# A gated feed-forward kernel with row-wise selection: the residual of blocks 0 to 2 added partly by accumulating transfers

## The reference

```
s_h = silu(xn @ Wg_a.T);  the 1376 entries of a row smallest in |s_h| are set to 0
s   = (s_h * (xn @ Wu_a.T)) @ Wd_a.T
g   = silu( (silu(xn @ Wg_b.T) * (xn @ Wu_b.T)) @ Wd_b.T )
out = x + s * g
```

## Time and profile before

| | us |
|---|---|
| median of 3 runs (lowest, highest) | 2768.76 (2768.42, 2770.05) |
| the profiled execution | 2768.99 |
| its span on the core | 2767.2 |

### The profile page before, as it was taken

How to read it: one execution, slowest core, us unless ns; L and a number is a source line. 1 busy time by engine, 2 the same in 40 slices (tenths; PEclk the granted TensorE clock), 3 DMA queues, 4 the chain that set the end, 5 groups by cost and what they waited for, 6 DMA issues and landing times.

```text
span 2767.2 us, 31398 instructions
## 1 busy us (share of the span) xinstructions
PE 2745.4 (99%) x12204; PEld 2275.1 (82%) x12204; DVE 2298.5 (83%) x3002; ACT 1350.6 (49%) x1386; POOL 408.4 (15%) x185
## 2 busy tenths in 40 slices
PE   9999999999999999999999999999999999999999
PEld 7878888878788888888878888888887888888887
DVE  6776989999976798998986688999898667999971
ACT  4235988332445477731145457771115546776110
POOL 5565443074400000000020000000011000000000
PEclk9999999999999999999999999999999999999999
DMA  6898888579766555556666655555666664555564
GB/s 234 313 337 286 294 288 278 211 265 362 256 195 192 179 192 197 192 190 223 245 205 191 193 179 197 189 191 197 243 220 205 193 196 180 188 193 198 191 232 169
DMA packets 135097, 614.28 MB, mean 222 GB/s; under 512 B 12752, under 2 KB 12752, under 8 KB 89168
## 3 DMA queue, kind: packets, MB, share of 16 engines
q1 hardware_dynamic: 134992, 612.94, 63.2%
HBM read 492.31 MB, written 120.59 MB: 221 GB/s over the span
## 4 chain that ended last, share of the span: by engine, by line
PE 88%; DVE 8%; DMA 2%; issue 1%; ACT 0%; POOL 0%; SPq 0%; DVEq 0%; POOLq 0%; ACTq 0%
PE ps L634 27%; PE ps L854 19%; PE ps L883 11%; PE ps L882 11%; PE ps L884 11%; PE ps L784 2%; PE ps L785 2%; PE ps L787 2%; DMA w_raw<-w_a 1%; DVE prods L1364 1%; DVE key_buf L1635 1%; DVE hid_ring L1407 1%; DVE xnT L1355 1%; DVE key_buf L1643 1%; DVE ranks L1605 1%
## 5 line engine op out<-in xcount | busy, mean ns | idle before, releaser
L634 PE MATMUL ps<-w_split,hid_ring 128*128 128x512 f32 x4096 | 933.7, 390 | 3.7 <-DVE hid_ring L1407 2.1
L634 PEld LDWEIGHTS ps<-w_split,hid_ring 128*128 128x128 f32 x4096 | 769.1, 188 | 167.2 <-issue 5.4
L1390 DVE TENSOR_SCALAR_CACHE_REDUCE ranks<-key_buf,cand 128x2752 int16<-128x2752 f32 x248 | 762.8, 3076 | 5.8
L968 ACT ACTIVATE signs_row<-key_buf,cand 128x2752 bf16<-128x2752 f32 x248 | 642.2, 2590 | 191.7 <-DVE cand L1399 182.2
L884 PE MATMUL ps<-xnT,w_split 128*128 128x512 f32 x1376 | 535.3, 389 | 0.0
L883 PE MATMUL ps<-xnT,w_split 128*128 128x512 f32 x1376 | 535.3, 389 | 0.0
L882 PE MATMUL ps<-xnT,w_split 128*128 128x512 f32 x1376 | 535.3, 389 | 0.0
L1216 POOL TENSOR_TENSOR w_split<-w_raw,w_split 128x1024 fp32r<-128x1024 f32 (+3 forms) x142 | 309.7, 2195 | 354.3 <-ACT w_split L935 134.6
L884 PEld LDWEIGHTS ps<-xnT,w_split 128*128 128x128 f32 x1376 | 258.3, 188 | 53.8
L882 PEld LDWEIGHTS ps<-xnT,w_split 128*128 128x128 f32 x1376 | 258.3, 188 | 53.7
L883 PEld LDWEIGHTS ps<-xnT,w_split 128*128 128x128 f32 x1376 | 258.3, 188 | 53.2
(11 more groups left out here) (146 smaller groups left out, 2884.6 us busy)
## 6 DMA issues: line engine op xcount, KB each, us to landing
w_split<-split SPq DMA_DIRECT2D x272, 1024.0 KB, 4.8
split<-w_split SPq DMA_DIRECT2D x72, 1024.0 KB, 6.7
w_raw<-w_a SPq DMA_DIRECT2D x97, 512.0 KB, 3.7
w_raw<-t_dram SPq DMA_DIRECT2D x81, 512.0 KB, 3.3
w_raw<-w_b SPq DMA_DIRECT2D x42, 512.0 KB, 4.8
t_dram<-t_buf SPq DMA_DIRECT2D x20, 1024.0 KB, 8.5
w_extra_raw<-t_dram SPq DMA_DIRECT2D x39, 512.0 KB, 3.3
w_extra_raw<-w_a SPq DMA_DIRECT2D x33, 512.0 KB, 3.6
```

Of the source, the lines that this page charges most:

```text
L634: ins = pe.matmul(ps[:, 2 * t + half, :], h, w[:, half * TB:(half + 1) * TB], start=(first and n == 0), stop=last and stop)
L968: act.activation(signs_row[:, :], keys[:, t, :], ACT.Sign, bias=cand_f[:, t:t + 1], scale=-1.0, accum_out=counts[:, t:t + 1]).then_inc(act ...
L1390: dve.tensor_scalar(ranks[:, :], keys[:, t, :], cand_f[:, t:t + 1], 0.0, ALU.is_lt, ALU.add, accum_out=counts[:, t:t + 1]).then_inc(sel_st ...
```

## The change

For blocks 0 to 2: x of row tiles 2 and 3 is no longer loaded into `x_res`, but copied by SP from `x` straight to its rows of `out` in DRAM. GpSimd makes the sums of row tiles 0 and 1 as before, and for row tiles 2 and 3 starts two transfers that add `silu_g` to what lies in `out` (`accum_op=ALU.add`, new semaphore `added`). DVE's `last_outputs` and SP's stores of row tiles 2 and 3 are gone. In block 3 nothing is computed in another way.

The homes of the token sums change: P6 goes to home 3 (now never written by x in these blocks), P5 to home 0, P7 to home 2, P3 to home 1. Their waits change with them: `s_hi(0)` waits for nothing of the block's end; `s_hi(1)` for GpSimd's two sums; `s_hi(2)` for the two stores; `s_hi(3)`, which stood with `s_hi(2)` at a = 5, stands at a = 7 and waits for both accumulating transfers.

```diff
+S_HOME = (3, 0, 2, 1)
...
-                    sp.dma_start(x_res[:, t, :], x_v[b][:, t, :]).then_inc(xres_landed[t], 16)
+                    dst = out_v[b][:, t, :] if b < NB - 1 and t >= STAGE else x_res[:, t, :]
+                    sp.dma_start(dst, x_v[b][:, t, :]).then_inc(xres_landed[t], 16)
...
                         if a == W_RING - 1:
                             store(b - 1, 0)
                             store(b - 1, 1)
-                        elif W_RING <= a < W_RING + 2:
-                            store(b - 1, a - W_RING + 2)
...
-                        return s_split[:, which, part, 2 * (1 - pair) + n, at_col:at_col + P]
+                        return s_split[:, S_HOME[which], part, 2 * (1 - pair) + n, at_col:at_col + P]
...
                             if a == 1:
-                                act.wait_ge(out_ready, (b - 1) * OUT_POOL + STAGE)
                                 s_hi(0)
                             elif a == 2:
-                                act.wait_ge(out_ready, (b - 1) * OUT_POOL + OUT_POOL)
-                                act.wait_ge(out_last, b)
+                                act.wait_ge(out_ready, b * STAGE)
                                 s_hi(1)
                             elif a == 5:
-                                act.wait_ge(stored, b * (16 * NT) + 16)
+                                act.wait_ge(stored, b * (16 * STAGE) + 16)
                                 s_hi(2)
+                            elif a == 7:
+                                act.wait_ge(added, b * (16 * (NT - STAGE)))
                                 s_hi(3)
...
-                for t in range(OUT_POOL if b < NB - 1 else OUT_POOL - 1):
+                for t in range(STAGE):
                     pool.wait_ge(xres_landed[t], b * 16 + 16)
                     pool.wait_ge(ad_free, b * NT + (NT + t + 1))
                     pool.tensor_tensor(x_res[:, t, :], x_res[:, t, :], silu_g[:, t, :], ALU.add).then_inc(out_ready, 1)
+                for t in range(STAGE, NT) if b < NB - 1 else ():
+                    pool.wait_ge(xres_landed[t], b * 16 + 16)
+                    pool.wait_ge(ad_free, b * NT + (NT + t + 1))
+                    pool.dma_start(out_v[b][:, t, :], silu_g[:, t, :], accum_op=ALU.add).then_inc(added, 16)
...
                     w_lows(b, 3, 4)
-                    last_outputs(b - 1, OUT_POOL)
```

More of the change, by code:

```diff
@@ L396, in build @@
         stored = sem("stored")
+        added = sem("added")
         sel_init = sem("sel_init")
@@ L557, in between @@
                     t = m - AD0 - 4 - NT
-                    sp.dma_start(x_res[:, t, :], x_v[b][:, t, :]).then_inc(xres_landed[t], 16)
+                    dst = out_v[b][:, t, :] if b < NB - 1 and t >= STAGE else x_res[:, t, :]
+                    sp.dma_start(dst, x_v[b][:, t, :]).then_inc(xres_landed[t], 16)
             def store(b, t):
[L561 to L564, removed]
+                sp.wait_ge(out_ready, b * STAGE + (t + 1))
                 sp.dma_start(out_v[b][:, t, :], x_res[:, t, :]).then_inc(stored, 16)
@@ L601, in _ @@
                 if t < OUT_POOL - 1:
-                    sp.wait_ge(out_ready, (NB - 1) * OUT_POOL + (t + 1))
+                    sp.wait_ge(out_ready, (NB - 1) * STAGE + (t + 1))
                 else:
-                    sp.wait_ge(out_last, (NB - 1) * (NT - OUT_POOL) + 1)
+                    sp.wait_ge(out_last, 1)
                 sp.dma_start(out_v[NB - 1][:, t, :], x_res[:, t, :]).then_inc(stored, 16)
@@ L607, in _ @@
                 cols = slice(half * TB, (half + 1) * TB)
-                sp.wait_ge(out_last, (NB - 1) * (NT - OUT_POOL) + (half + 2))
+                sp.wait_ge(out_last, half + 2)
                 sp.dma_start(out_v[NB - 1][:, NT - 1, cols], x_res[:, NT - 1, cols]).then_inc(stored, 16)
-            sp.wait_ge(stored, 16 * (NT * NB + 1) + 16)
+            sp.wait_ge(added, (NB - 1) * (16 * (NT - STAGE)))
+            sp.wait_ge(stored, 16 * ((NB - 1) * STAGE + NT + 1) + 16)
         @block.tensor
@@ L1032, in s_hi @@
                     act.wait_ge(s_raw, (b - 1) * 4 + 4)
-                    act.activation(s_split[:, which, 0, :, :].rearrange("p k n -> p (k n)"), prods[:, which, 0:H], ACT.Copy).then_inc(s_high, 1)
+                    act.activation(s_split[:, S_HOME[which], 0, :, :].rearrange("p k n -> p (k n)"), prods[:, which, 0:H], ACT.Copy).then_inc(s_high, 1)
                 if not first_block:
@@ L1071, in run @@
                         hi(b, m)
-                act.wait_ge(stored, b * (16 * NT) + 16)
+                act.wait_ge(stored, b * (16 * STAGE) + 16)
+                if not first_block:
+                    act.wait_ge(added, b * (16 * (NT - STAGE)))
                 def silu_b(c, rows=P, tiles=1):
@@ L1462, in s_lo @@
                     dve.wait_ge(s_high, (b - 1) * 4 + (which + 1))
-                    dve.tensor_tensor(s_split[:, which, 1, :, :].rearrange("p k n -> p (k n)"), prods[:, which, 0:H],
-                                      s_split[:, which, 0, :, :].rearrange("p k n -> p (k n)").bitcast(F32), ALU.subtract).then_inc(s_ready, 1)
+                    dve.tensor_tensor(s_split[:, S_HOME[which], 1, :, :].rearrange("p k n -> p (k n)"), prods[:, which, 0:H],
+                                      s_split[:, S_HOME[which], 0, :, :].rearrange("p k n -> p (k n)").bitcast(F32), ALU.subtract).then_inc(s_ready, 1)
                 def w_keys(s, tiles):
```

## The result

The changed kernel takes 2776.9 us, the median of 8 runs (2774.96 to 2778.66), against 2769.01 us (2768.24 to 2770.52) for the kernel before: 7.9 us slower, ratio 1.0024 with a 95% interval of 1.0015 to 1.0034. The forecast was 2764.0 us, with a range up to 2772.6 us: the measured time lies beyond it.

The account below looks back on a forecast made before the run. TensorE, busy 99% of the span, bounds the kernel; only its idle time at block starts, held by DVE's order, can be won. Gains of 1.88 + 1.44 + 1.44 = 4.8 us from 2768.76 give 2764.0 us, range 2762.5 to 2772.6.

Parts of the forecast that it names:

- the place of what could be won, and its size in blocks 2 and 3: At block starts, where TensorE idles: DVE's order makes P6 late; 1.44 us to win at each of blocks 2 and 3.
- the 4.8 forecast: Whole gain at the starts of blocks 1 to 3: 1.88 + 1.44 + 1.44 = 4.8 us.
- the 1.88 us of block 1: Start of block 1, from P1 on: P6 is 1.88 us late, all of it to be won.
- nothing waits for the accumulating transfers: Block starts: only `s_hi(3)` on ACT waits for the two adding transfers, which land in time; cost 0.
- 5.8 to 17 us was bounded, 19.6 allowed: Block 2 start: both adding transfers take 5.8 to 17 us; they must land within 19.6 us of GpSimd's second sum.
- Rival B: Before P2: adding transfers land too late, `s_hi(3)`, `s_lo(3)` and TensorE wait; slower, 2770 to 2795 us; chance 0.11.
- Rival A: Block starts: GpSimd's issue blocks DVE's subtractions as a sum does; 2766.4 us, or 2772.6 if both issues do; chance 0.18.
- the copies in DRAM cost nothing to be seen: Copying x to out instead of loading it to SBUF: taken as 0, with bounds of 0 to 3 us.
- "Their traffic ... Cost 0": Block 2 start: adding transfers read 1 MB more, but weight loads may take over three times as long; cost 0.
- The allowance: Block 2 start: weight tile 8, asked for at about 1415.8, has its raw data wanted at 1427.0.
- Rival C: Before P6: another late arrival, say slower weight loads from two extra reads, replaces DVE's chain; nothing won, 2768.8 us; chance 0.08.
- T1: Theory for the experiments: adding makes transfers dear in DMA engine time, delaying weight loads they meet; for e4, 2770 to 2775 us.

Follow-up runs that it names:

- e2: Changed kernel, but GpSimd starts no transfer for row tiles 2 and 3, only counts the semaphore up; 2766.84 us, ratio 0.9986 to the kernel before.
- e6: Kernel before, but DVE sums row tiles 2 and 3 behind weight tile 5's low part; later stores, new homes, no adding transfers; 2767.88 us, ratio 0.9989.
- e10: The kernel of e6 run again, unchanged, on another chip's comparison with the kernel before; 2766.76 us, ratio 0.9990.
- e7: The kernel before, run again unchanged for a second profile; 2769.62 us.
- e1: Changed kernel, but GpSimd's transfers of row tiles 2 and 3 write silu_g to out without adding; 2767.11 us, ratio 0.9991 to the kernel before.
- e3: Changed kernel, but the adding transfers carry only the first 512 of 1024 columns of each row; 2769.39 us, ratio 0.9996 to the kernel before.
- e4: Changed kernel, but SP's two stores moved from behind the load of weight tile 5 to behind that of tile 7; 2780.44 us, ratio 1.0032.
- e8: The changed kernel, run again unchanged for a second profile; 2776.47 us, ratio 1.0025 to the kernel before.

## Why the prediction was wrong

**Right: the place of what could be won, and its size in blocks 2 and 3.** Only the starts of the blocks had idle time on TensorE. xn_low 7 lasted 0.68 us instead of 2.89 with no sum of GpSimd beside it, and P6 began on the beat. In e2 block 2 and block 3 win 1.44 us each, as summed. In e6 the whole is 2037.9 - 2032.9 = 5.0 us against the 4.8 forecast.

**Too large: the 1.88 us of block 1.** In e2 and e10 the whole is only 3.5 us, and by the medians e2, e6 and e10 win 3.0, 2.6 and 2.9 us. The term was read from one profile in which P4 of block 1 had waited 1.99 us. Where the wait was 2.08 us (e6), P4 took 5.59 us and the term came true: P4 to P6 is 11.13 us against 12.91. In e2 and e10 P4 began after waits of 3.18 and 2.96 us and took 7.17 and 7.20 us, and P4 to P6 is 12.61 and 12.64 us. In the kernel before such a slow P4 costs nothing: in e7 it took 7.20 us and P4 to P6 is 12.88 us, since DVE's chain held P6 back anyway. So the term is worth 1.8 us or 0.3 us, by the wait that happens to stand before P4.

**Right: nothing waits for the accumulating transfers.** GpSimd's issues in the changed kernel (L1276, ns min/median/max, and the time to landing):

```profile
L1276 POOL DMA_DIRECT2D out<-hid_buf x6: 848/1074/1177, 735.2 to 2094.2; - x6
...
DMA to landing us min/median/max: 8.1/10.3/12.7
```

Both run at once, so the pair had landed some 12 us after the second sum; 5.8 to 17 us was bounded, 19.6 allowed. ACT goes into `s_hi(3)` at 1432.85 without an idle time. Rival B, which forecast a slower kernel, named the wrong wait.

**Right: GpSimd's issue does not block DVE.** xn_low 6 and 7 of block 2 in the changed kernel (L1361, ns min/median/max, starts):

```profile
L1361 DVE TENSOR_TENSOR xnT<-prods,xnT x2: 680/1432/2183, 1412.6 to 1414.7; 128x512 fp32r<-128x512 f32 x2
```

xn_low 7, from 1414.7 on, ran beside GpSimd's issues (1414.20 to 1415.95) in 680 ns; in blocks 1 and 3 it took 681 and 679 ns. Rival A is out. This agrees with what the Trainium skill (SBUF — State Buffer, Who interferes with whom) says and marks as inferred.

**Right: the copies in DRAM cost nothing to be seen.** e2 has them and e10 has not, and their ratios to the kernel before are 0.9986 and 0.9990, with intervals that overlap.

**Wrong: "Their traffic ... Cost 0".** This step failed, in three ways, and the rest of the loss follows from it.
- The price of a transfer was counted in bytes: one more MB read. The profile does not even count such a read (492.31 MB read from HBM before and after, and in e1). In engine time a packet that adds costs 0.36 us against 0.19 us for the plain one (e1). The two transfers take 288 x 0.36 / 16 = 6.5 us of all 16 engines; the two stores they replace, at 0.163 us a packet (86.6% of 16 x 12 us over 1022 packets), 2.9 us for as many packets. At a place where the engines were in use for 86.6% of 12 us, 1.6 us were free for the 3.6 us more. Why a packet that adds holds its engine longer, no run shows.
- GpSimd's transfers go through a queue of their own, and it held the engines for a little over half of the time (54.2%), the loads' queue for 41.5%. So the loads did not go first: those of tiles 6 and 7 took 10.4 us in the median and those of 8 and 9 9.3 us, instead of the 4.5 and 5.4 us before. The prediction's 3.3 us, a median over the whole run, was too low for this place from the start.
- The allowance was worked out for weight tile 8 alone, 11 us. Tile 6 is the tight one: asked for at 1412.13 of the kernel before, behind the second store, and wanted by P5 at 1418.33 + 5.44 = 1423.77. Back from there by the high part (1.06), the low part (1.15) and `s_lo(1)` (1.14) it must have landed by 1420.4: 8.3 us, not 11. It took 9.4 us (1414.68 to 1424.09). Tile 7, asked for 0.9 us later, took 11.5 us and made P7 late.

The late loads cost 1.72, 3.36 and 3.38 us in the three blocks of the changed kernel's profile, 8.5 us in all; the gain up to P6 was 0.29 us in block 1 (P4 to P6 12.62 us against 12.91, since P4 took 7.18 us) and 1.44 in each of the others, 3.2 us. The difference, 5.3 us, is the 5.2 us of the table within rounding. In the second profile the loss is 7.5 us; there P7 of block 2 came late by 3.2 us and ran 1.7 us longer, and P4 of block 1 ran 1.1 us longer than in the first.

Rival C, "slower weight loads from the two extra reads", came nearest to the mechanism, but it looked for the late load before P6, where nothing was late, and was sized to give back the gain and no more, with a chance of 0.08 and no case beyond it. It should have been worked out like B, from the tightest load, with the adding bounded in engine time.

## What to carry to other kernels

A transfer that is off every chain still has a price: the engine time it takes from the transfers that are on one. So find the load with the least time between its request and its use in the stretch where the new traffic runs, and hold its landing time under a crowded DMA against that, not the median of the whole run. And an addition in a transfer saves an engine's instruction but here costs about twice a plain transfer's DMA time; moving the instruction to where its engine has time kept the gain (e6, e10), and the same traffic moved to where the loads had slack cost 2 us instead of 11.

## What the runs showed of the hardware beyond the question

A packet of GpSimd's queue kept its DMA engine for 0.36 us when adding in DRAM and for 0.19 us when writing plainly, 0.22 us when adding half as much; counted by the 4 KB packets (2 KB in e3) alone these are 0.41, 0.21 and 0.25 us. From issue to landing an adding transfer of 512 KB took 8.1 to 12.7 us, a plain one 5.2 to 8.3 us. GpSimd needed 1.07 us (median) to issue an adding transfer, 0.55 us for a plain one.

TensorE's granted clock fell behind some waits. The busy times by stretch of e4 for P7 and of e6 for P4 of block 1 (from:to, length, PE, PEld, DVE, ACT, POOL busy, clock, DMA share, GB/s):

```profile
1437.60:1445.90 8.30, 8.29 (x25) 6.59 (x26) 3.15 (x3) 2.97 (x4) 0.00 (x0) 0.65 0.19 65
```

```profile
733.30:738.90 5.60, 5.57 (x24) 4.47 (x25) 5.60 (x5) 1.72 (x3) 4.77 (x2) 1.00 0.36 146
```

In the first TensorE had idled for 2.98 us before, and the 24 matmuls took 8.27 us at 0.65 of the full clock, so in part at the lower of its two levels (1.2 of 2.4 GHz); in the second it had idled for 2.08 us, the clock stayed at 1.00, and they took 5.59 us. In these profiles P4, P6 and P7 behind waits of up to 2.33 us took 5.5 to 5.6 us, behind waits of 2.53 to 3.63 us 6.9 to 8.3 us. (The wait of 2.53 us, before P7 of block 2 in e8, had one of 0.5 us inside the P5 before it.) So a wait that grows a little can cost 1.4 to 2.8 us more than itself; no run changed such a wait alone. In e4 the three P7 took 7.14, 8.27 and 6.89 us, some 6 us more in all than three times 5.44 us; e4's median lies 5.4 us above T1's range. Of the 2.3 us between the two profiles of the changed kernel, P4 of block 1 (8.27 us against 7.18) and P7 of block 2 (7.16 against 5.52) make 2.7 us, and late loads give 0.4 us back.
